# A transformer block on one core: feed-forward products as three fp32r passes, and a new order of the stages

## The reference, cut to what matters

```python
def attn_layer(x, Wqkv, qs, ksc, Wo):      # 16 heads of 64, INNER = 1024
    q, k, v = split(x @ Wqkv)
    q, k = l2norm(q) * qs, l2norm(k) * ksc  # then rotary tables
    out = local_attention(q, k, v)          # windows of 32, each sees itself and the one before
    return out @ Wo

def ffn_layer(x, g, bln, W1, b1, W2, b2):   # DIM_INNER = 341
    xn = layernorm(x) * g + bln
    a, gate = jnp.split(xn @ W1 + b1, 2, -1)
    return a * gelu(gate) @ W2 + b2

for i in range(6):
    x = attn_layer(shift_tokens(x), ...) + x
    x = ffn_layer(shift_tokens(x), ...) + x
```

## Time and profile before

| | |
|---|---|
| median of the runs | 3269.31 us |
| profiled execution, its own time | 3271.82 us |
| span of its profile | 3270.0 us |
| mean granted TensorE clock | 0.993 |
| PE busy | 3202.3 us, 98% |
| DVE, ACT, POOL busy | 2647.7, 2431.3, 2213.2 us |

### The profile page before, as it was taken

The page is one execution under the profiler, slowest core; times in us unless marked ns, Lnnn a source line. Parts: engine busy times, 40 slices in busy tenths (PEclk is TensorE's granted clock), DMA queues, the critical chain, the costliest instruction groups (busy, mean ns, idle before and its releaser), DMA issues. The chain is left out here.

```text
span 3270.0 us, 149708 instructions
## 1 busy us (share of the span) xinstructions
PE 3202.3 (98%) x62645; PEld 2538.3 (78%) x62645; DVE 2647.7 (81%) x6351; ACT 2431.3 (74%) x5028; POOL 2213.2 (68%) x1332
## 2 busy tenths in 40 slices
PE   7889999999999999999999999999999999999997
PEld 5668877877887887787787788778788778778875
DVE  5658888878888887888888888888888888888884
ACT  3347777777777777777777778778777777777774
POOL 5448767766776776676776677677677667767762
PEclk9989999999999999999999999999999999999999
DMA  4431111221211131111122111122111122112111
GB/s 160 161 128 51 45 43 43 55 88 48 56 46 42 47 98 48 53 45 43 46 87 63 48 50 46 38 82 71 49 44 48 43 62 87 53 45 53 50 45 37
DMA packets 110574, 200.00 MB, mean 61 GB/s; under 512 B 19280, under 2 KB 40784, under 8 KB 109136
## 3 DMA queue, kind: packets, MB, share of 16 engines
q1 hardware_dynamic: 107168, 185.17, 19.6%
q10 hardware_dynamic: 2736, 5.25, 0.5%
HBM read 41.45 MB, written 23.07 MB: 20 GB/s over the span
## 5 line engine op out<-in xcount | busy, mean ns | idle before, releaser
L438 POOL TENSOR_TENSOR qks<-work 128x1024 f32<-128x1024 f32 x384 | 909.9, 2370 | 134.9 <-issue 125.5
L446 POOL TENSOR_TENSOR qkr<-qks,rnorm 128x1024 f32<-128x1024 f32 x384 | 731.5, 1905 | 310.4 <-issue 223.0
L789 PE MATMUL psum<-wparts,xhi 128*128 128x512 f32 x2304 | 821.8, 438 | 11.9 <-POOL xlo L423 7.0
L573 ACT ACTIVATE sq<-psum 128x512 f32<-128x512 f32 x768 | 459.9, 599 | 301.4 <-PE psum L789 280.4
L454 POOL TENSOR_TENSOR probn<-prob,psumr 128x512 f32<-128x512 f32 x384 | 401.5, 1046 | 370.7 <-DVE psumr L1170 370.5
L1119 DVE TENSOR_REDUCE ssq<-sq 128x8 f32<-128x512 f32 x768 | 519.9, 677 | 4.3 <-ACT sq L573 4.2
L1146 DVE TENSOR_TENSOR work<-psum,rot 128x512 f32<-128x512 f32 x768 | 509.1, 663 | 1.8 <-POOL qks L438 1.8
L814 PEld LDWEIGHTS psum<-kT,qTs 64*32 64x32 f32 x24576 | 360.5, 107 | 145.2 <-issue 129.8
L789 PEld LDWEIGHTS psum<-wparts,xhi 128*128 128x128 f32 x2304 | 384.7, 191 | 101.2 <-issue 50.2
L789 PE MATMUL psum<-wparts,xlo 128*128 128x512 f32 x1152 | 459.7, 399 | 0.0
L1164 DVE TENSOR_REDUCE psumr<-prob 128x8 f32<-128x512 f32 x384 | 261.7, 682 | 243.4 <-ACT prob L625 240.8
(11 more groups left out here) (132 smaller groups left out, 5536.7 us busy)
## 6 DMA issues: line engine op xcount, KB each, us to landing
vsh<-vtok SPq DMA_DIRECT2D x384, 192.0 KB, 2.4
vsh<-vtok SPq DMA_DIRECT2D x384, 64.0 KB, 2.4
wsplit<-wstage SPq DMA_DIRECT2D x15, 1024.0 KB, 6.4
wparts<-wsplit SPq DMA_DIRECT2D x30, 512.0 KB, 3.9
xsh<-xs_in SPq DMA_DIRECT2D x192, 64.0 KB, 2.4
ff_x<-x_mid SPq DMA_DIRECT2D x96, 128.0 KB, 2.4
wraw<-Wqkv_dram SPq DMA_DIRECT2D x18, 512.0 KB, 4.3
rsplit<-rstage SPq DMA_DIRECT2D x5, 1024.0 KB, 3.8
```

The source lines that it names most:

```text
L438: pool.tensor_tensor(qks[:, :, :], rcos, rsin, ALU.add).then_inc(s["add_ready"], 1)
L446: pool.tensor_tensor(qkr[:, n % 2, :, :], qks[:, :, :], rnorm[:, :].unsqueeze(2).to_broadcast([P, 2 * OCT, DH]), ALU.mult).then_inc(s["qkr ...
L573: act.activation(sq[:, w * OCT:(w + 1) * OCT, :], bank[w].rearrange("p (h n) -> p h n", n=DH), ACT.Square).then_inc(s[("sqq_ready", "sqk_r ...
L789: mm = pe.matmul(out, xparts[xp][:, ti, :], wparts[:, SECTION_AT[w, oc], wp_, :], start=(k == 0), stop=(k == 2))
```

## The change

1. Feed-forward products take three fp32r passes, as the projections do. `W1` and `W2` of a layer lie side by side in `Wff` (1066 columns), and are split in the global stage as a fourth piece per layer (24 pieces); `w1` and `w2` become `wff` with `hi` and `lo`. ACT and POOL split the activations: `ffn_high` and `ffn_low` for `ff_n`, `gated_high` and `gated_low` for `gel`, one instruction for each of its three chunks.
2. Each engine's loop has another order and other delays. The pipe is longer: scores at `step - 4`, turn_probabilities at `step - 7`, attend and output at `step - 8`, and the feed-forward part reaches from place 1 to place 7 (down, out), with ACT's and POOL's calls at places of their own.

```diff
-PIECES = len(SECTIONS) // 2
+PIECES = len(SECTIONS) // 2 + 1
+FFW = 2 * DFF + CH * D
...
 def block_at(step, place):
-    b = step // UNROLL - 2
-    return b if step % UNROLL == place and 0 <= b < DEPTH * BLOCKS else None
+    b = (step - place) // UNROLL - 2
+    return b if (step - place) % UNROLL == 0 and 0 <= b < DEPTH * BLOCKS else None
...
+            for step in range(STEPS + 3 * UNROLL):          # SP
                 x_half(step)
...
-                values_shifted(step - 4)
+                values_shifted(step - 7)
...
+                section_renewed(renewed_at(step, 0), SECTION_AT[0, 0])
+                section_renewed(renewed_at(step, 0), SECTION_AT[1, 0])
+                section_renewed(renewed_at(step, 1), SECTION_AT[0, 1])
+                section_renewed(renewed_at(step, 1), SECTION_AT[1, 1])
...
+                section_renewed(renewed_at(step, 4), SECTION_AT[2, 0])
+                section_renewed(renewed_at(step, 5), SECTION_AT[2, 1])
+                output_renewed(renewed_at(step, 9))
...
-            for n, pieces in ((1, 2), (2, 3), (3, 3), (4, 3), (5, 3), (6, 4)):
+            for n, pieces in ((1, 4), (2, 4), (3, 4), (4, 4), (5, 4), (6, 4)):
...
-            x_low(0)
             global_inverse(2 * B - 1)
...
+            def ffn_low(b):
...
+                pool.wait_ge(s["f_xh"], b + 1)
+                pool.tensor_tensor(ff_lo[:, :], ff_n[:, :], ff_hi[:, :].bitcast(F32), ALU.subtract).then_inc(s["f_xl"], 1)
...
+            def gated_low(b):
...
+                    pool.wait_ge(s["f_uh"], b * CH + ch + 1)
+                    pool.tensor_tensor(gel_lo[0:w, ch, :], gel[0:w, ch, :], gel_hi[0:w, ch, :].bitcast(F32), ALU.subtract).then_inc(s["f_ul"], 1)
...
+            for step in range(STEPS + 3 * UNROLL):          # POOL
+                normed(step - 4)
+                x_low(step - 2)
+                rotated(step - 3)
+                probabilities(step - 8)
+                gated_low(block_at(step, 8))
+                ffn_low(block_at(step, 4))
...
+                act.wait_ge(s["f_xnT"], b + 1)
+                act.activation(ff_hi[:, :], ff_n[:, :], ACT.Copy).then_inc(s["f_xh"], 1)
...
+                    act.wait_ge(s["f_u"], b * CH + ch + 1)
+                    act.activation(gel_hi[0:w, ch, :], gel[0:w, ch, :], ACT.Copy).then_inc(s["f_uh"], 1)
...
-                act.dma_start(w1[:, :], W1[layer]).then_inc(s["w1_in"], 16)
-                act.dma_start(w2[:, :, :].rearrange("p k n -> p (k n)"), W2[layer]).then_inc(s["w2_in"], 16)
+                act.dma_start(wff[:, :, :].bitcast(F32).rearrange("p h n -> p (h n)"), wsplit[layer - 1, PIECES - 1]).then_inc(s["wff_in"], 16)
...
+            for step in range(STEPS + 3 * UNROLL):          # ACT
+                ffn_renewed(renewed_at(step, 16))
+                x_high(step)
+                q_turned(step - 3)
+                values(step - 5)
+                exponential(step - 5)
+                attended(step - 8)
+                ffn_gates(block_at(step, 3))
+                probabilities_turned(step - 7)
+                k_turned(step - 3)
+                square(step, 0)
+                ffn_affine(block_at(step, 2))
                 mask_seeded(step - 3)
+                ffn_high(block_at(step, 2))
+                ffn_inverse(block_at(step, 1))
                 inverse_norm(step - 1)
+                gated_high(block_at(step, 3))
                 square(step, 1)
...
+                    for k, (xp, wp_) in enumerate(PARTS):   # ffn_up; ffn_down alike
+                        mm = pe.matmul(bank[FFN_BANKS[ch]][0:w, :], wff[:, wp_, DFF + ch * P:DFF + ch * P + w], ff_parts[xp][:, :],
+                                       start=(k == 0), stop=(k == 2))
...
+            for step in range(STEPS + 3 * UNROLL):          # PE
+                turn_q(step - 3)
+                scores(step - 4)
+                attend(step - 8, block_at(step, 4))
+                ffn_up(block_at(step, 3), step)
+                turn_probabilities(step - 7, ...)
+                turn_k(step - 3)
                 projection(step, 0)
+                ffn_features(block_at(step, 2), step)
+                turned_back(last_block_at(step, 8), step)
+                ffn_tokens(block_at(step, 1), step)
+                output(step - 8)
                 projection(step, 1)
+                ffn_down(block_at(step, 7), step)
+                value_projection(step - 4)
...
+            for step in range(STEPS + 3 * UNROLL):          # DVE
+                probability_sum(step - 5)
+                square_sum(step - 1, 1)
+                below_maximum(step - 4)
+                added(last_block_at(step, 9))
+                ffn_statistics(block_at(step, 1))
+                scaled(last_block_at(step, 8))
                 inverse_sum(step - 5)
                 guarded(step - 1)
+                ffn_gated(block_at(step, 3))
+                residual(step - 8)
+                square_sum(step, 0)
+                ffn_normed(block_at(step, 1))
+                rotation(step, 0)
+                rotation(step, 1)
+                ffn_out(block_at(step, 7))
+                row_maximum(step - 3)
```

More of the change, by code:

```diff
@@ L102, in build @@
         ff_x = sb("ff_x", [P, BLK])
-        ff_n = sb("ff_n", [P, BLK])
-        gel = sb("gel", [P, CH, BLK])
+        ff_n = shared("ff_n", [P, BLK])
+        ff_lo = sb("ff_lo", [P, BLK], F32R)
+        ff_hi = sb("ff_hi", [P, BLK], F32R)
+        ff_parts = (ff_hi, ff_lo)
+        gel = shared("gel", [P, CH, BLK])
+        gel_lo = sb("gel_lo", [P, CH, BLK], F32R)
+        gel_hi = sb("gel_hi", [P, CH, BLK], F32R)
+        gel_parts = (gel_hi, gel_lo)
         gel_flat = gel[:, :, :].rearrange("p c n -> p (c n)")
@@ L398, in _ @@
             pool.wait_ge(s["gvs_ready"], 2)
-            for layer in range(4):
+            for layer in range(DEPTH - 1):
                 rotary_gains(layer)
@@ L402, in _ @@
             pool.wait_ge(s["gxn_ready"], 2)
-            for layer in range(4, DEPTH):
-                rotary_gains(layer)
+            rotary_gains(DEPTH - 1)
             done = 0
-            for n, pieces in ((1, 2), (2, 3), (3, 3), (4, 3), (5, 3), (6, 4)):
+            for n, pieces in ((1, 4), (2, 4), (3, 4), (4, 4), (5, 4), (6, 4)):
                 if n > 1:
@@ L455, in probabilities @@
                                    ALU.mult).then_inc(s["pn_ready"], 1)
[L457 to L462, removed]
+            for step in range(STEPS + 3 * UNROLL):
[5 more added lines that the diff above has]
+                ffn_low(block_at(step, 4))
         @block.scalar
@@ L643, in ffn_affine, with ffn_high, gated_high @@
                                bias=lnb_col[:, layer:layer + 1]).then_inc(s["f_xnT"], 1)
+            def ffn_high(b):
+                if b is None:
+                    return
+                act.wait_ge(s["f_xnT"], b + 1)
+                act.activation(ff_hi[:, :], ff_n[:, :], ACT.Copy).then_inc(s["f_xh"], 1)
+            def gated_high(b):
+                if b is None:
+                    return
+                for ch in range(CH):
+                    w = CW[ch]
+                    act.wait_ge(s["f_u"], b * CH + ch + 1)
+                    act.activation(gel_hi[0:w, ch, :], gel[0:w, ch, :], ACT.Copy).then_inc(s["f_uh"], 1)
             def ffn_gates(b):
@@ L938, in ffn_up, with ffn_down @@
                     pe.wait_ge(s["f_gel"], b * CH + ch + 1)
[L939 to L942 removed]
+                    for k, (xp, wp_) in enumerate(PARTS):
+                        mm = pe.matmul(bank[FFN_BANKS[ch]][0:w, :], wff[:, wp_, ch * P:ch * P + w], ff_parts[xp][:, :],
+                                       start=(k == 0), stop=(k == 2))
+                    mm.then_inc(s["f_a"], 1)
+            def ffn_down(b, step):
                 if b is None:
                     return
[L945 to L947 removed]
+                pe.wait_ge(s["f_ul"], b * CH + CH)
+                need(pe, "pts_ready", min(step - 6, STEPS))
                 for ch in range(CH):
[L949 removed]
+                    w = CW[ch]
+                    for k, (xp, wp_) in enumerate(PARTS):
+                        mm = pe.matmul(bank[4], w2[0:w, wp_, ch, :], gel_parts[xp][0:w, ch, :], start=(ch == 0 and k == 0), stop=(ch == CH - 1 and k == 2))
                 mm.then_inc(s["f_y"], 1)
```

142 lines of the change are left out of this document (51 added, 91 removed).

## The result

The changed kernel takes 3371.7 us (median of 4 runs, 3367.6 to 3373.1) against 3270.5 (4 runs): ratio 1.031, interval 1.030 to 1.032. I had forecast 3197, in a range of 3150 to 3262. It is slower, where I had said faster, and outside the range. The profiled execution took 3371.3 us, its span 3369.5, 99.5 more than before.

What follows compares the result with a forecast made beforehand. PE, busy 98% of the span, was taken to set the pace. From 3271.8 us profiled, -67 - 77 + 48 + 11 + 12 = -73 gave 3199, or 3197 us against the median; range 3150 to 3262.

Steps and rivals of the forecast that it cites:

- The new order on PE: PE's reordered step, summed from old-trace intervals: 5.64 us against 5.85 per even step, 77 us saved over 384 steps.
- Scores to attend: PE interval between these groups, not in the old trace; taken as 1.03 us, from scores to turn_q.
- my rivals: Scores to attend free (0.15), order saves little (0.22), order saves nothing (0.08), POOL's lump exposed and kernel slower (0.12).
- Rival (d): Slower: POOL's lump is exposed, up to 5.1 us a block; 3341 us with 3 us exposed; chance 0.12.
- POOL's lump: On POOL, gated_low as one 3.8 us piece ahead of normed and rotated; forecast expected nothing seen of it.
- Products, -67: Feed-forward products on PE: three fp32r passes make nine products 1.4 us a block shorter, 67 us over 48 blocks.
- Order, -77: PE's new step order: three changes of array parts instead of four, 0.20 us a step, 77 us over 384 steps.
- up's lost cover and lumps, +48: Per block, 0.9 us waiting for gelu without the output product's cover, plus 0.1 for added element-wise work; 48 us.
- The 0.9 us for up: PE's wait per block in up, which now follows attend directly, for gelu and ACT's late copy; between 0.4 and 2.0.
- Global stage, +11: Weight splitting before the main stage: six more pieces delay two inverses; 11 us later, bounds 0 and 16.
- x_low(0): First POOL subtraction for the projections, now behind the last inverse of the global stage; priced at 1 us.
- Filling, draining, tail, +12: Pipe two steps deeper: 8 us of idle PE and cold clock, 3 to 4 in the serial last block; bounds 4 and 25.

Runs made afterwards that it cites:

- run 8: Run 5's kernel with DVE's three gating operations ahead of that step's sum of probabilities instead of behind it; 3217.0 us, ratio 0.983.
- run 5: Kernel before with three-pass products in its own order, weight-splitting pieces placed 5, 3, 5, 3, 5, 3 between POOL's inverses; 3250.9 us, ratio 0.994.
- run 6: Changed kernel with weight-splitting pieces placed 5, 3, 5, 3, 5, 3 between POOL's inverses instead of 4 each; 3357.0 us, ratio 1.027.
- run 10: Run 6's kernel with only every other pair of attend's matmuls issued, 32 of 64 per unit; 3226.2 us, ratio 0.987.
- run 1: Changed kernel with the transposes of k (turn_k) moved between scores and attend on PE; 3411.7 us, ratio 1.044.
- run 4: Changed kernel with each feed-forward product back to one fp32 matmul on the rounded parts, splitting kept; 3420.4 us, ratio 1.046.
- run 7: Changed kernel with bursts of scores and attend matmuls added after the last output; single execution, first-series period 3.70 us from the third burst on.

## Why the prediction was wrong

**The step that failed** stands in "The new order on PE": "I add it from intervals with the same neighbours". Each interval was right. Scores to attend is 1.03, an even step 5.65 against 5.64. What I left out, a term put at nothing without a reason, is that intervals taken from different places of the old order hold only if PE gets its instructions as fast as the new order uses them. The old order kept the two dense groups apart: scores until 1258.11, then 2.85 us of transposes and projections, then attend at 1260.96. Side by side they use 256 instructions in 2.1 us, while packets of 256 start at least 3.2 us apart and PE goes on only 2.2 to 2.9 us after one has started. The stops that follow, some 107 us in attend, are most of the 144 us. None of my rivals was about that. Rival (d), the slower one, had POOL's lump, and that didn't happen: the waits of PE show POOL nowhere in front. Its 3341 us is nearer the result than my forecast, for a reason that wasn't there.

Term by term:
- Products, -67: right, in the order of the kernel before. Undisturbed blocks of 62.51 before and 61.13 in run 8 differ by 1.38 us, where I had 1.4.
- Order, -77, with up's lost cover and lumps, +48: the undisturbed block, 60.74 for 60.6, bears them out. The 0.9 us for up, of the 48, was right as well. Up takes 5.21 us from its first start to the next group's (median) and 4.27 in run 8, so 0.94 is lost. In the timeline below, the second gate product starts 1.27 us after the first where 0.70 is a product, and the first a product 1.13 us after the third gate; the brackets show less, as they count from the modelled ends:

```profile
1255.30 0.74 PE L981 MATMUL psum<-ff_hi,wff 128*128 128x512 f32 x2
...
1256.57 0.71 PE L981 MATMUL psum<-ff_hi,wff 128*128 128x512 f32 x2 [0.31 <-ACT aoT L574]
...
1257.35 0.62 PE L981 MATMUL psum<-ff_hi,wff 128*85 128x512 f32 x2
...
1258.48 0.73 PE L988 MATMUL psum<-ff_hi,wff 128*128 128x512 f32 x2 [0.27 <-ACT gel L694]
...
1260.66 0.60 PE L893 MATMUL psum<-ident,probn 128*128 128x128 f32 x4
```

- Scores to attend from 1.03: the 64 launches of scores take 0.88, and the other 0.15 is paid although attend, too, works on parts of the array. The Trainium skill ("TensorEngine Tiling (Array Packing)", "Key Properties") has it so, and the trace agrees.
- Global stage, +11: it was 20.8, beyond my upper bound of 16. I had named the mechanism, the fourth piece ahead of two inverses; the size was short. Runs 5 and 6 give 8 us back by moving the pieces. Whether x_low(0), which I had priced at 1, counts for more is not shown: run 6's first P0 (232.8) waits for it, behind the last inverse, and run 5's, with x_low(0) ahead of that inverse, stands 6 us earlier (226.8), but run 10, with the global stage of run 6, starts at 225.9.
- Filling, draining, tail, +12: 14.4, within its bounds.
- Missing: +144 in the blocks. Without it the changed kernel would take 3371 - 144 = 3227 us, inside my range, and run 10 shows a kernel with nearly that pace at 3226.

The change as a whole loses because its two halves have opposite signs: the products are worth 62 us of blocks (45 x 1.38), the order costs more than it gives. Of the order's own gain 0.4 us a block is left where nothing stops (60.74 against 61.13), and the blocks lose 3.2 us each (144 over 45) to stops, waits and the half clock.

The half clock comes with PE's long idle stretches, whoever causes them. From 300 to 3180 us the changed kernel and runs 1, 4, 6, 7 and 10 have 69 spells, and each follows or overlaps an idle stretch of 1.26 us or more. The other six kernels, with no idle stretch above 1.23 us there, have no spell. The spells shrink with the stops (61.4 to 17.1 us from run 6 to run 10, 47.8 to 20.5 from the changed kernel to run 1). What stays open is why some such stretches bring a spell and others none, and why the start of the main stage differs by up to 8 us between kernels with the same global stage.

## What to carry to other kernels

Before putting two groups of small matmuls side by side, count their instructions, weight loads included, and the time in which they would pass: here 256 in 2.1 us starved PE, and 256 in 2.8 us, once per step, hardly did (1.3 us of stops in attend). A wait "for issue" in the middle of a group without a semaphore is the sign; look then for the packet of the instruction queue some 2.5 us earlier, and whether the instructions between two stops are a multiple of 256. A change of products and a change of order belong in two kernels, since here the first was worth 1.7% with two small repairs (runs 5 and 8), and the second hid it.

## What the runs showed of the hardware

- PE's instructions come in packets of 16,384 bytes, 256 each (128,725 over 503; run 10 has 407 packets, also 256 each). Some 251 of them are matmuls and weight loads. When PE has run out, it goes on 2.2 to 3.0 us after a packet's start, with or without other traffic; no two packets start within 3.2 us, and a lasting demand gets one per 3.7 us, some 14 ns an instruction (3.7 us over 256).
- The 64 attend matmuls start in fours, one on each 64x64 part of the array, 7 ns apart within the four. They take 0.92 us from first start to last, and the 32 on one half of the columns alone take 0.90. The Trainium skill ("TensorEngine Tiling (Array Packing)", "Key Properties") says that tiles of the array work in parallel, and run 10 agrees.
- PE's granted clock fell from 1.00 to 0.50 in the middle of the main stage, though PE was busy 93% of the span: 12 spells in the changed kernel, each beginning during or within 2 us after an idle stretch of PE of 1.35 to 3.5 us. In the kernel before and in run 8, whose longest idle stretches are 1.1 us, it was 1.00 throughout this stage.
